# A six-sublayer decoder on one core: the same steps merged into new engine orders, with new PSUM places

## The reference

```
x = ln(x + attn0(x))             # 16 heads of 16, rotary positions, softmax
x = ln(x + mlstm(x, ctx, ctx))   # 8 heads of 32: D = exp(cumulated gates), (q k^T * D) v / max(|sum|, e^-m), head norm
x = ln(x + ffn0(x))              # ternary weights, 8-bit activations, relu(gate)^2 * up, inner size 1024
x = ln(x + attn1(x))             # 16 heads of 16, softmax
x = ln(x + xattn1(x, ctx, ctx))  # cross attention to ctx, 16 heads of 16
x = ln(x + ffn1(x))              # relu MLP, inner size 1024
```

## Time and profile before

| | |
|---|---|
| median of three runs | 1808.5 us (1807.71 to 1810.19) |
| profiled execution, first to last instruction | 1806.2 us |
| TensorE busy with matmuls | 1566.7 us, 87% |
| VectorE busy | 1172.7 us, 65% |
| ScalarE busy | 965.5 us, 53% |
| GpSimd busy | 227.6 us, 13% |
| mean granted TensorE clock | 0.951 of full |

### The profile page before, as it was taken

One profiled execution on the slowest core, in us unless ns is written; L12 is line 12 of the kernel. 1 busy time (PEld: TensorE's weight loads), 2 busy tenths in 40 slices (PEclk: granted clock), 3 DMA queues, 4 the chain that ended last, 5 costly groups with the idle time before them and its releaser, 6 DMA issues.

```text
span 1806.2 us, 31799 instructions
## 1 busy us (share of the span) xinstructions
PE 1566.7 (87%) x12524; PEld 999.6 (55%) x12546; DVE 1172.7 (65%) x2087; ACT 965.5 (53%) x1717; POOL 227.6 (13%) x233
## 2 busy tenths in 40 slices
PE   7489778989998887889999898888899889798898
PEld 4246545546665464555676465555566556464467
DVE  4946687664456678786347678886355668887722
ACT  1177454555444764555544674655445566555662
POOL 4200110001121111000112102000022111100000
PEclk9579799989999999999999999998999999899999
DMA  6620023220231011322121101332123101132100
GB/s 213 188 60 1 1 67 102 76 74 31 74 91 54 2 42 42 105 81 74 59 71 48 48 7 36 91 103 74 33 71 98 56 1 42 42 104 83 63 1 24
DMA packets 115747, 114.36 MB, mean 63 GB/s; under 512 B 10514, under 2 KB 101394, under 8 KB 115602
## 3 DMA queue, kind: packets, MB, share of 16 engines
q1 hardware_dynamic: 115282, 111.28, 20.2%
q10 hardware_dynamic: 320, 1.05, 0.3%
HBM read 68.91 MB, written 42.99 MB: 62 GB/s over the span
## 4 chain that ended last, share of the span: by engine, by line
PE 55%; DVE 15%; ACT 7%; DMA 7%; issue 4%; SPq 1%; POOL 0%; DVEq 0%; ACTq 0%
PE psum L686 9%; PE psum L796 7%; PE psum L931 6%; PE psum L679 5%; DVE nm L1169 5%; PE psum L923 5%; PE psum L759 4%; DMA heads_dram<-U 4%; PE psum L778 3%; ACT PB L998 3%; PE psum L673 2%; PE psum L719 2%; DMA QK<-heads_dram 2%; PE psum L807 2%; PE psum L863 2%
## 5 line engine op out<-in xcount | busy, mean ns | idle before, releaser
L1169 DVE TENSOR_REDUCE nm<-psum 128x4 f16<-128x1024 f32 x384 | 456.7, 1224 | 124.6 <-PE psum L759 122.7
L998 ACT ACTIVATE PB<-psum 128x1024 f32<-128x1024 f32 x384 | 383.7, 1024 | 236.6 <-PE psum L796 124.3
L1344 POOL TENSOR_TENSOR XO<-XO,row_b 128x512 f32<-128x512 f32 x80 | 102.9, 1290 | 1165.8 <-ACT XT L969 1144.6
L796 PE MATMUL psum<-PB,V 128*32 128x256 f32 x3072 | 214.6, 398 | 17.9 <-ACT PB L998 14.7
L759 PE MATMUL psum<-QK 48*128 48x256 f16 x1536 | 149.6, 291 | 65.1 <-DVE nm L1169 23.6
L778 PE MATMUL psum<-QK 49*128 49x256 f16 x1536 | 149.0, 282 | 33.7 <-ACT PB L998 9.2
L759 PEld LDWEIGHTS psum<-QK 48*128 48x128 f16 x1536 | 55.5, 97 | 157.5 <-issue 60.5
L796 PEld LDWEIGHTS psum<-PB,V 128*32 128x32 f32 x3072 | 84.7, 112 | 98.8 <-issue 37.3
L778 PEld LDWEIGHTS psum<-QK 49*128 49x128 f16 x1536 | 52.4, 96 | 132.4 <-issue 60.3
L923 PE MATMUL psum<-XT,W 128*128 128x256 f32 x512 | 122.3, 388 | 0.6 <-ACT XT L969 0.5
L931 PE MATMUL psum<-W,PB 128*128 128x256 f32 x512 | 116.1, 382 | 0.0
(11 more groups left out here) (158 smaller groups left out, 2585.1 us busy)
## 6 DMA issues: line engine op xcount, KB each, us to landing
QK<-heads_dram SPq DMA_DIRECT2D x96, 512.0 KB, 3.6
heads_dram<-U SPq DMA_DIRECT2D x288, 128.0 KB, 2.0
XO<-in_x SPq DMA_DIRECT2D x16, 256.0 KB, 2.9
Y<-in_ctx SPq DMA_DIRECT2D x16, 256.0 KB, 3.8
out<-XO SPq DMA_DIRECT2D x16, 256.0 KB, 3.6
W<-in_w SPq DMA_DIRECT2D x2, 1024.0 KB, 6.9
QK<-GN SPq DMA_DIRECT2D x96, 4.0 KB
heads_dram<-QK ACTq DMA_DIRECT2D x4, 256.0 KB, 8.9
```

The costliest lines, as they stand in the source:

```text
L796: ins = pe.matmul(b[SLOT * j:SLOT * j + SLOT, at:at + TOK], value(L, t, PAIRS * e + u, HEADS, HD, SLOT), src, start=(t == 0), stop=(t == T ...
L998: act.activation(PB[L][:, unit % PBUF, :], b[:, 0:1024], ACT.Exp, scale=HD ** -0.5)\
L1169: dve.tensor_reduce(nm[L][:, :, :, unit].rearrange("p t e -> p e t"), b[:, 0:1024].rearrange("p (e t k) -> p e t k", e=2, t=TT), AX.X, ALU ...
L1344: pool.tensor_tensor(stream(L, it), stream(L, it), row_b[:, occ:occ + 1, :].to_broadcast([P, TT, DIM]), ALU.add).then_inc(xb_ready[L], 1)
```

## The change

`TURNS` and `PLACES` are new tables; not a line of code is changed. The steps, the buffers, the semaphores and the count each wait asks for are the same. Which TensorE step frees a bank for which other follows from the new tables. Two lines of each table, from the start:

```diff
 TURNS = {
     "pe": (
-        "0001231020112332200332313422110003300022020221112220112133311032313330000010030222200222023023030233230"
+        "0000122013331222004112233110000000032223222211111123302133123031033000030021222000220322020233032330"
...
     "dve": (
-        "0123001420203142243100013003200202221112221113311333333444000200223330220132311032132032001301003203"
+        "2000422004111223331100000000223232222111112133131333334444000200232330202131231032130232001301030303"
...
     "sp": (
-        "0011223340002022121134313344204134000033330222121113020003123302322131121001300020300233331312222322"
+        "2330400001220221121113333201344400003333402222111312000013333042222131121001000330020233333121222232"
...
 PLACES = (
-    "5313275036135737453650371516460526024662206242427463026406206246042630460264240520620470425060254127"
+    "6416543051273271264152535403046405240260250306140265173460422461240624076402506420260472530234105731"
```

129 lines of the change are left out of this document (64 added, 65 removed).

## The result

The changed kernel takes 1701.68 us in the median (1697.73 to 1707.49), against 1808.11 us for the kernel before on the same chips: a ratio of 0.941, 95% interval 0.9378 to 0.9443. That is 106 us less; 25 were predicted, and the time lies far outside the range. A second set of runs gave 1700.51 us and 0.9399 (0.9374 to 0.9425). All ratios leave out executions more than 1.5% above the fastest of their kernel: one of `refined_again`, and two of the kernel before beside `plain_search` and `banks_only`.

The account below looks back on a forecast made before the run. The run was taken as mostly the sum of TensorE's step costs, with VectorE leading in some stretches. Terms 13 + 8 + 3 + 1 = 25 us off 1808.5 gave 1783 us; 8-in-10 range 1764 to 1804.

Parts of the forecast that it names:

- Part 1: TensorE, whole run: 138 fewer tile changes save 18 us of its work, 13 us of it at the end (10 to 20).
- Parts 2 and 3: First attention: first `ternary` behind the maxima on VectorE, maxima ahead of weights on SP; together 8 us (3.7 to 10.1).
- part 3: SP in the first attention: turned maxima issued ahead of the weight loads, landing about 4.5 us earlier; 3.7 us alone.
- Part 4: TensorE's waits for readers and banks, counted from distances in its order: 6 us back, 3 lost, net 3 us gained.
- Part 5: Granted clock, 115 us at half clock beyond the first attention: 1 us gained, bounds -12 and +12.
- Savings turn into idle time: Rival, chance 0.15: shorter TensorE steps only wait for VectorE and ScalarE; 1800 to 1805 us.
- pairs flood VectorE: Rival, chance 0.12: more two-step stretches of `max` and `exp` make TensorE wait for VectorE; slower, 1832 us.
- The clock stays up too: Rival, chance 0.18: a fifth of the 115 us is warm, 11 us more, or part 1 comes whole; 1765 to 1772 us.

Follow-up runs that it names:

- refined_again: Second run of a kernel whose orders and banks start from `plain_search` and are refined with every tile change counted: 1695.74 us, ratio 0.9359 to the kernel before.
- plain_search: Kernel before with all five engines' orders and the banks found anew by a search counting neither tile changes nor clock: 1741.59 us, ratio 0.9637.
- banks_only: Kernel before with its five orders kept and only the PSUM banks found anew (595 of 1777 uses keep theirs): 1828.87 us, ratio 1.0114.
- less_v: Kernel before with one of four products left out in each of the 48 `v` steps, 20.6 us less TensorE work: 1796.69 us, ratio 0.9927.
- exc_v: Changed kernel with a small 48-row product inside each of the 48 `v` steps, 96 more tile changes: 1714.52 us, 12.8 us above the changed kernel.
- tern_only: Kernel before with only the first `ternary` moved behind the 32 maxima of the first attention on VectorE: 1807.26 us, ratio 1.0009.
- sp_only: Kernel before with only SP's order taken from the changed kernel, turned maxima ahead of the weight loads: 1813.51 us, ratio 1.0034.
- s_head: Kernel before with the changed kernel's orders and banks for TensorE's first 100 steps and part of the other engines' new orders: 1804.09 us, ratio 0.9994.
- s_half: Changed kernel's orders and banks on all engines up to TensorE's step 950, those of the kernel before from there on: 1739.42 us, ratio 0.9619.
- pe_new: Changed kernel's TensorE order and banks, with the other engines as near to the orders of the kernel before as possible: 2131.52 us, ratio 1.1794.
- long_plain: Kernel before with all orders and banks found anew, like `plain_search` but by a longer search, tile changes and clock uncounted: 1729.48 us, ratio 0.9567.
- long_counted: Same start, length and moves as `long_plain`, but each tile change counted as TensorE time, 188 fewer changes: 1722.65 us, ratio 0.9531 to the kernel before.

## Why the prediction was wrong, by its own steps

**Part 1, the tile changes: right.** "I take 18 us of TensorE's work": the priced sum fell by 18.7 us (146.4 to 127.7), and the prices hold in the changed kernel. There an L931 step between steps of other tiles takes 846.14 - 842.49 = 3.65 us in its timeline:

```profile
842.49 3.72 PE L931 MATMUL psum<-W,PB 128*128 128x256 f32 x16
846.14 0.22 PE L768 MATMUL psum<-ident,nm 128*16 128x128 f16 x1
```

Against 3.66 in the earlier trace rows. "Not all of it reaches the end ... I take 13": `less_v` and `exc_v` delivered 66% and 50% of TensorE's time, which is 12 and 9 of 18.7 us. By the interval of `less_v`, 39% to 89%, it is 7 to 17 us, so the 13 fits. This term was the subject of most of the working and is an eighth of the result.

**Parts 2 and 3, the head: right at the head; what it is worth at the end is open.** The first `exp` came at 82.50 us and step 100 came 11.0 us earlier, where 8 were taken. Taken alone, neither move reached the end: `tern_only` and `sp_only` ended 2 us above and 6 above the kernel before (their ratios times 1808), where 4 to 6 and 3 to 4 below were expected. `s_head` (1 below) lacks part 3 and says nothing of the two together. In `s_half` the head stayed with the orders that follow it, and there the lead grew. That an early start survives only if the orders behind it fit agrees with this and is not shown by itself.

**Part 4, the waits: the step that failed.** "Net 3 us gained; bounds -6 and +6" was 66 us. Two errors made it. First, the pool, the sum of waits from which a share was taken, was too small: I scaled 23.6 and 14.7 us, rows of single releasers, where all waiting together was 280 us. It could have been had from the prediction's own figures. TensorE was idle for 1806.2 - 1566.7 = 239.5 us, and the chain gave 45% to others; a bound had to come from this sum. Second, the count was of the distance between a reader's producer and TensorE's step, in TensorE's order alone. How late a reader is depends on what stands ahead of it on its own engine, and on what that waited for. `pe_new` settles this: with TensorE's order and banks, and so every distance that I had counted, as in the changed kernel, the waiting was 502 us and not 215.

**Part 5, the clock: failed with part 4.** "I take 1 us, with bounds of -12 and +12": 22.9 us, by 69 us less at half clock. The sentence "Whether the new order keeps the clock up the rows cannot tell" was true, but the two terms do not look independent. Over the ten kernels of the table more waiting broadly goes with more half clock, from 204 us with 112 to 502 us with 463. If the waits bring the half clock, a gain in waits is paid out more than once, by about a third on top here (22.9 to 65.7), and the range had to be stretched by it. That the one makes the other is argued: no run changed the waits alone. `exc_v`, with more work for TensorE, had the higher clock.

**The rivals.** "Savings turn into idle time" and "pairs flood VectorE" did not come: VectorE's idle time in front of the maxima fell by 28 us with more of the two-step stretches. "The clock stays up too" had the right direction, and a size of 11 us. The case that came, that waits and clock fall together by 89 us, was not on the list, though the new tables of all five engines were in plain sight in the change. The word-for-word places shown from the orders were a few rows of thousands, and such a place tells what moved, not what the move is worth. (The chance of a time below 1804.9 us, 0.50 + 0.18 + 0.05 + two thirds of 0.15, is 0.83 and not 0.82.)

**What is settled and what is open.** Shown are the price of a tile change and, roughly, what part of it reaches the end; that TensorE's order with the banks, SP's order and the first `ternary` do not carry the gain alone, the first of them losing 326 us; and that a joint refit of orders and banks gives 66 to 79 us without fewer changes. Not shown is how the 66 us divide over the engines' orders, since the orders were tried apart only in part, and how much of the changed kernel's lead of 28 us over `long_plain` comes from its counting of changes, its counting of the clock, or a longer search. By the table that lead is 27 us of changes, 7 of clock and -4 of waiting, but `long_counted` shows that counting does not have to bring this.

## What to carry to other kernels

When a change rewrites the order of several in-order engines at once, bound its effect by all the time in which the busiest engine waits, plus what the clock may give back with it, and not by the waits into a few kinds of step; the counted resource may be the smallest term. Never judge one engine's order apart from the others': here TensorE's half of a good set made the kernel 18% slower, and two plausible local swaps that save a few tenths cost a microsecond. Fit the orders together, and price each swap with the reader's own queue in it.

## What the runs showed of the hardware that was not expected

- A wait of 1.77 us was followed by a piece of half clock, in which eight matmuls took 3.29 us instead of 1.93, and the steps from the `max` ahead of the wait to the `pv` behind it took 346.56 - 340.80 = 5.76 us instead of 334.88 - 332.32 = 2.56. Where such pieces fall shifts with changes far ahead of them.
- The same program differed by 8.7 us between two executions, mostly through such pieces; and `exc_v`, with more work than the changed kernel, had the higher clock. With 26 us between the fastest and the slowest of 29 executions of the kernel before, effects of a few us can't be read from one execution of this kernel.
- The first `ternary` not only moved, it became shorter: 2.15, 2.01 and 2.18 us before, 1.28, 1.23 and 1.23 us in the changed kernel for the same three instructions. GpSimd and the DMA engines differ: the first of these windows is the kernel before during them, the second the changed kernel. GpSimd's L1344 beside them took 2.25 us, as the third row shows from its timeline, where 80 of these take 1290 ns in the mean of the same kernel. So both engines were slower together. `pe_new` tells the two apart: there the three instructions run beside transfers (DMA share 0.83) with GpSimd idle, and take 1.27, 1.23 and 1.23 us, as the fourth and fifth row show. So it is GpSimd beside them that makes them longer, not the transfers. The Trainium skill (SBUF — State Buffer, SBUF: two separate sides) has engines and DMA apart, and lets certain VectorE instructions contend with GpSimd for one shared pair of ports, held exclusively for a whole instruction; the traces agree with both.

```profile
47.80:54.30 6.50, 2.55 (x12) 1.73 (x12) 6.43 (x5) 2.08 (x3) 6.50 (x4) 0.60 0.90 277
```

```profile
89.50:93.30 3.80, 3.09 (x30) 1.14 (x26) 3.73 (x4) 2.31 (x3) 0.00 (x0) 0.50 0.00 0
```

```profile
50.91 2.25 POOL L1344 TENSOR_TENSOR XO<-XO,row_b 128x512 f32<-128x512 f32 x1
```

```profile
54.30:58.20 3.90, 3.75 (x5) 1.58 (x6) 3.74 (x4) 0.00 (x0) 0.00 (x0) 0.50 0.83 213
```

```profile
54.32 1.27 DVE L1136 TENSOR_SCALAR W_gu<-W_gu,w_scale 128x2048 f32<-128x2048 f32 x1
```

- Entering the 128 by 128 tile costs 0.10 to 0.11 us with a dense float32 step and about 0.05 us with a transpose, entering the 64-row tile about 0.01; leaving costs 0.10. These are start-to-start distances at full clock, usual over the traces: a second half of a feed-forward step (L931) takes 3.45 us between steps of its own tile, 3.55 with a 64-row step behind it, 3.56 with one ahead and 3.65 with both; a float32 transpose step (L673) 0.44, 0.53, 0.49 and 0.59. The bfloat16 `down` step (L686) pays only some 0.01 us for a 64-row step ahead, 1.757 instead of 1.745. With the prices of the table and the steps' own work, 1301 us of the span are work in every kernel here, and what orders can change in the kernel before lies in the other 490 us (changes, half clock and waiting), of which the changed kernel still has 383.
